# A layer of gated state-space mixing beside a hashed mixture of experts, on one core: chunks transposed from where they lie, GpSimd's tile loop turned round, and the additions of x placed elsewhere

## What is computed

```python
xn = LN(x)                                     # no gain, no bias
# mixing: hidden width 256, state 16
u  = xn @ W_x.T + b_x
g  = sigmoid(xn @ W_g.T + b_g)
u  = u * g + (conv3(u) + conv_b) * (1 - g)     # 3 taps along the sequence
dt = clip(softplus(xn @ W_dt.T + b_dt).mean over all tokens, 0.001, 2)
A  = -softplus(A_raw);  A_d = exp(A * dt);  B_d = (A_d - 1) / (A + 1e-6) * B_ssm
s_t = A_d * s_{t-1} + B_d * u_t;  y_t = sum_s(s_t * C_ssm)
a  = LN(xn + y @ W_out.T + b_out) * ln_g + ln_b
# experts: 8, hidden 512; each token goes to two neighbours, h and h + 1 (mod 8)
h  = int(xn[0] + xn[1]) mod 8
f  = 0.5 * (expert_h(xn) + expert_{h+1}(xn)),  expert_e(v) = relu(v @ W1[e] + b1[e]) @ W2[e] + b2[e]
out = x + a + f
```

## Time and profile before

| | us |
|---|---|
| median of three runs | 494.08 |
| the three runs | 494.71, 491.63, 494.08 |
| the profiled execution, its own time | 491.58 |
| its span, first to last instruction | 489.8 |

### The profile page before, as it was taken

One profiled execution on the slowest core, in us unless ns is written; L12 is line 12 of the kernel. 1 busy time (PEld: TensorE's weight loads), 2 busy tenths in 40 slices (PEclk: granted clock), 3 DMA queues, 4 the chain that ended last, 5 costly groups with the idle time before them and its releaser, 6 DMA issues.

```text
span 489.8 us, 10915 instructions
## 1 busy us (share of the span) xinstructions
PE 423.6 (86%) x3463; PEld 375.1 (77%) x3463; DVE 381.3 (78%) x594; ACT 323.4 (66%) x932; POOL 246.3 (50%) x274
## 2 busy tenths in 40 slices
PE   1056799999889999999999899899999999899940
...
GB/s 237 261 407 324 123 156 181 170 104 141 70 54 32 44 43 43 39 36 43 80 43 43 84 37 132 72 72 43 43 43 33 216 118 152 58 250 148 203 109 128
DMA packets 81254, 56.53 MB, mean 115 GB/s; under 512 B 6178, under 2 KB 74826, under 8 KB 81226
## 3 DMA queue, kind: packets, MB, share of 16 engines
...
## 4 chain that ended last, share of the span: by engine, by line
issue 32%; PE 27%; DVE 12%; DMA 12%; POOL 11%; ACT 3%; POOLq 1%; DVEq 0%; ACTq 0%; SPq 0%
DMA sorted_tokens<-RA,posi 11%; PE PS L1378 8%; POOL AR L580 5%; POOL sorted_tokens L550 3%; PE PS L1445 3%; PE PS L1442 2%; PE PS L1451 2%; DVE RC L1168 2%; PE PS L1361 2%; PE PS L1363 2%; PE PS L1362 2%; PE PS L1428 2%; DVE RC L856 2%; DVE AR L1182 2%; PE PS L1421 1%
## 5 line engine op out<-in xcount | busy, mean ns | idle before, releaser
L1378 PE MATMUL PS<-AR 128*128 128x128 f32 x1184 | 138.5, 275 | 2.3 <-ACT AR L747 2.3
L1378 PEld LDWEIGHTS PS<-AR 128*128 128x128 f32 x1184 | 135.1, 192 | 2.7 <-ACT AR L747 2.7
L747 ACT ACTIVATE AR<-PS,VC 128x256 f32<-128x256 f32 x296 | 112.3, 491 | 10.0 <-PE PS L1363 10.0
L1361 PE MATMUL PS<-XT,RR 128*128 128x256 f32 x296 | 86.2, 291 | 6.5 <-POOL RR L576 3.5
L1363 PE MATMUL PS<-XT,RR 128*128 128x256 f32 x296 | 82.8, 280 | 0.0
L1362 PE MATMUL PS<-XT,RR 128*128 128x256 f32 x296 | 82.5, 279 | 0.0
L556 POOL TENSOR_TENSOR XT<-XTF,XT 128x256 fp32r<-128x256 f32 x37 | 33.3, 900 | 97.8 <-ACT XT L720 97.8
L550 POOL DMA_INDIRECT sorted_tokens<-RA,posi x64 | 61.8, 966 | 23.3 <-issue 13.3
L756 ACT ACTIVATE AR<-PS 128x128 f32<-128x128 f32 x74 | 16.5, 275 | 71.5 <-PE PS L1378 67.8
L580 POOL TENSOR_TENSOR AR<-AR,b2p 128x256 f32<-128x256 f32 x37 | 35.2, 953 | 55.9 <-ACT AR L756 55.6
L1361 PEld LDWEIGHTS PS<-XT,RR 128*128 128x128 f32 x296 | 55.8, 188 | 7.9 <-POOL RR L576 3.9
...
## 6 DMA issues: line engine op xcount, KB each, us to landing
...
AR<-sorted_tokens SPq DMA_DIRECT2D x39, 128.0 KB, 2.1
sorted_outputs<-AR SPq DMA_DIRECT2D x37, 128.0 KB, 1.8
...
```

The lines of the kernel that those rows point to most:

```text
L747: nc.scalar.activation(HID[n][:, k, :], ps[2 * n + k // 2][:, (k % 2) * FT:(k % 2 + 1) * FT], ACT.Relu, bias=B1C[:, e, k:k + 1]).then_inc( ...
L1361: T.matmul(bank, W1h[slot][:, w], XT[:, 0:FT], start=True, stop=False)
L1378: ins = T.matmul(ps[5 + h][:, 0:D], HID[n][:, k, h * P:(h + 1) * P], W2S[slot][:, k, :], start=(n == 0 and k == 0), stop=(n == 1 and k == ...
```

## The change

Line numbers in this section's rows are those of the kernel before or after, as said.

- **Chunks in place.** `transpose_chunk` reads `XN` itself and waits for the norm's pieces; the DMA copies to `xin` are gone, and TensorE's loop over the chunks is written out instead of looped. SyncE's loop only stores chunks, from turn 0 on, and waits for the chunk that it stores to be transposed. The zero tile moves from `RC` to `AR[:, 0:2 * CH]`, where `xin` was, and has 8 blocks, so 11 + 3 clearing DMAs take the place of 9 + 2. ScalarE no longer waits for the clearing; SyncE does, before it loads the first W2. VectorE's `low(1, 0)` goes ahead of the ranking.
- **GpSimd's tile loop.** It does `low_part(i + 1)` first and then the bias; VectorE's `low_tile(1)` is gone, since GpSimd's first turn now makes that part.
- **Exponentials.** `ER` is taken at g = 3 instead of g = 2, with a wait of VectorE's of its own.
- **In-chunk matrix.** In each half of `INTRA`'s rows only the 64 columns of that half are other than zero; it is packed to these 64 columns; the three large memsets become 24 of 512 columns.
- **Gathers.** All are plain, NPL = 4. Batches 4 to 7 go to the half of `RB` that the packing frees, where before 4 to 7 were in the other half; x for batches 0 to 3 is loaded into that same half first, and GpSimd waits for its addition (`s_xb`) before it gathers there.
- **Additions of x and gains.** In the scan stage `add_x` comes at q = 6, 10 and 13 (before at q = 8, 11 and 14); in the tail at g = 2, 3, 7, 11 and 15. `VG` shrinks from six groups to four, so ScalarE scales groups 5 and 9.

```diff
@@ -379,29 +377,23 @@
-            sp.wait_ge(s_nrm, 1)
-            sp.wait_ge(s_nra, 1)
-            for s in range(2):
-                sp.dma_start(xin[s], XN[:, s * TPC:(s + 1) * TPC, :]).then_inc(s_xin[s], 16)
...
-            with sp.Fori(1, NCH // 2) as i:
+            with sp.Fori(0, NCH // 2) as i:
                 for s in range(2):
-                    sp.wait_ge(s_xt[s], i)
-                    sp.dma_start(xin[s], XN[:, bass.ds((i * 2 + s) * TPC, TPC), :]).then_inc(s_xin[s], 16)
+                    sp.wait_ge(s_xt[s], i + 1)
                     sp.dma_start(xn_v[:, bass.ds((i * 2 + s) * TPC, TPC), :], XN[:, bass.ds((i * 2 + s) * TPC, TPC), :]
                                  ).then_inc(s_xnd, 16)
@@ -424,8 +416,9 @@
             sp.dma_start(XSIN, xs_v[0]).then_inc(s_xs, 16)
+            sp.wait_ge(s_fill, 16 * NZ)
+            sp.wait_ge(s_fily, 16 * NY)
             for s in range(2):
-                sp.wait_ge(s_xt[s], NCH // 2)
                 load_w2(s)
@@ -576,10 +569,10 @@
                 with pool.Fori(bounds[g], bounds[g + 1]) as i:
+                    low_part(i + 1)
                     pool.wait_ge(s_ysb, i + 2)
                     nc.gpsimd.tensor_tensor(YSB, YSB, b2p[:, :].rearrange("p (o d) -> p o d", o=1).broadcast_to([P, FH, D]),
                                             ALU.add).then_inc(s_yad, 1)
-                    low_part(i + 2)
@@ -590,15 +583,13 @@
             for n in range(NB8):
-                if n not in PLAIN:
-                    pool.wait_ge(s_xg[n], 16)
-                elif n >= NAR:
-                    pool.wait_ge(s_yps, PPB)
+                if n >= NAR:
+                    pool.wait_ge(s_xb, n - NAR + 1)
...
-                                                 compute_op=ALU.bypass if n in PLAIN else ALU.add).then_inc(s_gat[n], 16)
+                                                 compute_op=ALU.bypass).then_inc(s_gat[n], 16)
@@ -669,8 +660,6 @@
-            act.wait_ge(s_fill, 16 * NZ)
-            act.wait_ge(s_fily, 32)
@@ -731,7 +720,8 @@
-                    nc.scalar.activation(EX, EX, ACT.Exp)
+                    nc.scalar.activation(EX, EX, ACT.Exp).then_inc(s_eexp, 1)
+                if g == 3:
                     nc.scalar.activation(ER, ER, ACT.Exp).then_inc(s_eexp, 1)
@@ -1023,9 +1012,6 @@
-            dve.wait_ge(s_ws, 2)
-            low_tile(1)
@@ -1109,15 +1095,16 @@
-                    ins = V.tensor_copy(IN5[r, hb, :, q, :], TT[r, hb])
+                    ins = V.tensor_copy(IN5[r, hb, :, q % 2, :], TT[r, hb])
@@ -1181,11 +1168,9 @@
-                if q >= DPB and (q - DPB) % 3 == 0 and (q - DPB) // 3 < NPL:
-                    add_x((q - DPB) // 3)
+                if q in (DPB - 2, DPB + 2, DPB + 5):
+                    add_x((q - DPB + 2) // 3)
@@ -1229,8 +1214,14 @@
+                if g == 2:
+                    add_x(3)
+                if g in (3, 7, 11):
+                    add_x(g // 4 + 4)
                 if g + 1 == NT // 4:
+                    scale_gain(13)
                     gain(NB8 - 2)
+                    add_x(NB8 - 1)
@@ -1263,11 +1263,14 @@
             def transpose_chunk(s, i):
-                pe.wait_ge(s_xin[s], (i + 1) * 16)
...
+                pe.wait_ge(s_nrm, q + 1)
+                pe.wait_ge(s_nra, q + 1)
...
-                    ins = T.transpose(ps[s][:, t * P:(t + 1) * P], xin[s][:, t, :], identity[:, :])
+                    ins = T.transpose(ps[s][:, t * P:(t + 1) * P], XN[:, t0 + t, :], identity[:, :])
```

70 lines of the change are left out of this document (31 added, 39 removed).

## The result

Over 20 runs each, the changed kernel takes 491.14 us (median), the kernel before 493.61 us: a ratio of 0.9949, with a 95% interval of 0.9930 to 0.9969. That is 1.5 to 3.5 us faster. One of the changed kernel's 20 runs, 527.01 us at a mean granted clock of 0.845, belongs to a slow state and is left out of the ratio; without it the median is 490.84 us. The forecast was 488.4 us, a gain of 5.65 us; the time is inside the range, but the gain is 2.5 us by the medians and 1.3 us in the profiled pair.

What follows compares the result with a forecast made beforehand. TensorE was taken to bound the kernel until about 375 us, VectorE later, alone from 470.69. Terms +4.7 + 1.6 - 3.1 - 1.0 - 4.0 - 1.0 - 2.85 = -5.65 us gave 488.4 us from 494.08; range 483.5 to 493.0.

Steps and rivals of the forecast that it cites:

- head, to the last chunk: Chunk stage: without the chunk copies and clearing wait, the last chunk's transposes come 2.6 us earlier (bounds 0 and 4.8).
- first sorted tile (from the last chunk on): Before the first sorted tile: SyncE's later loads make TensorE stand 7.3 us, a 4.7 us loss with the head gain included.
- clock behind the stand, to the first tile's products: After TensorE's stand before the first sorted tile: a low granted clock costs 1.6 us (bounds 0 and 3.2).
- tiles 0 to 2: Start of the expert loop: a gain of 3.1 us from tile 0 on, 0.8 if GpSimd's small operations take 4.4.
- boundaries: Between experts: 1.0 us from moving one exponential and 4.0 from GpSimd making the first weights' low part earlier, sum 5.0.
- scan stage: Scan stage: the first of three additions of x moves into VectorE's idle slot, gaining 1.0 us (bounds 0 and 1.2).
- tail: VectorE's last stretch: three additions of x leave (3.8 us), four activations cost 1.0; gain 2.85 (bounds 1.8 and 3.8).
- the next transposes come at 55.4: Head: after ScalarE's high part at 52.8 us, TensorE's next transposes come at 55.4 instead of 57.97 us, gaining 2.6.
- inside the head's slack: Head: the old 4.80 us stand and its 1.6 us clock loss cost nothing, since ScalarE sets the pace there.
- rival (b): Six expert boundaries: GpSimd's new order delays the next low part 1.4 us each, 8.4 in all; 500.8 us, chance 0.08.
- GpSimd releasing TensorE in the middle of the loop: Expert loop: a sign that the forecast is wrong, if VectorE or GpSimd ends TensorE's waits there; no size given.
- the stand at the first tile: Before the first sorted tile's transposes: TensorE idle some 7.3 us, ended by that tile's DMA; under 4 us means wrong.

Runs made afterwards that it cites:

- e2: Changed kernel, but TensorE loads its eight tile bounds before the first sorted tile instead of among the first chunks: 489.76 us, ratio 0.9946 to the kernel before.
- e5: Changed kernel with TensorE's bounds loaded late and chunk 3 transposed twelve times over while TensorE has nothing to do: 490.65 us, ratio 0.9945 to the kernel before.
- e3: Changed kernel without GpSimd's three small operations for the pair's bias, except for the first pair: 489.44 us, ratio 0.9914 to the kernel before.
- e1: Changed kernel, but SyncE loads tile bounds and block counts ahead of its loop of stores instead of behind it: 495.05 us, ratio 1.0037 to the kernel before.
- e7: Changed kernel with the tail's additions of x and the six scale-and-gain groups at their places of before: 492.60 us, ratio 0.9977 to the kernel before.
- e12: Changed kernel with the scan stage's three additions of x back at steps 8, 11 and 14: 493.39 us, ratio 0.9990 to the kernel before.

## Why the prediction was wrong

No step had the wrong sign. The sum promised 4.35 us more than the profiled pair gave, and 3.2 more than the medians of 20 runs; against the 488.4 us forecast, which started from the median of three runs, the median is 2.7 us high. By its steps, forecast against profile:

| step | forecast | measured |
|---|---|---|
| head, to the last chunk | -2.6 | -0.2 |
| first sorted tile (from the last chunk on) | +7.3 | +7.8 |
| clock behind the stand, to the first tile's products | +1.6 | +1.2 |
| tiles 0 to 2 | -3.1 | -3.0 |
| boundaries | -5.0 | -3.2 |
| scan stage | -1.0 | -1.2 |
| tail | -2.85 | -2.75 |
| sum | -5.65 | -1.3 |

Each measured value is the difference of two marks. The first two lines are 107.95 against 108.12, and 12.32 against 4.55 us from there to the first tile. Then come 6.97 against 5.74 us to its products, and 17.97 against 20.94 from there to the third tile's mark. The boundaries are 228.0 against 231.2 from there to the last, the scan stage 63.65 against 64.84 (to the first scales), and the tail 46.22 against 48.97. They sum to -1.3.

**The step that failed first is "the next transposes come at 55.4" in the head.** ScalarE did come at 53.12 (forecast 52.8). I followed ScalarE alone and did not ask what TensorE does in the meantime. It has eight loads of its own there: the stand of 4.80 us gave way to one of 4.46 us behind them, and the low clock that I had written off as "inside the head's slack" now fell on products that were needed. Nor were these loads the only cause, since e2, without them there, stood 5.20 us for ScalarE's and had the low clock too. It cost 1.86 us from the high part on (1.2 in other profiles of the same head), which e5 shows by keeping the clock up. So 1.9 of the 2.4 us missing in the head are this. The wait that was removed here did not take its clock loss with it.

**The second is in the boundaries.** The W1 part's waits went fully (4.2 us of a forecast 4.0), the exponential gave 0.95 of 1.0, as intervals of the tiles. But 2.0 us came back at two boundaries (1.1 in some of the other profiles), where the next low part stood behind small operations and W1 part. That was rival (b)'s mechanism, priced for six boundaries, and one of the prediction's own signs of being wrong, GpSimd releasing TensorE in the middle of the loop. It acted at two of the six. At the first, GpSimd's operations were drawn out beside VectorE's, and e3, without the small operations, has no wait there.

**Right in size, though not what it seemed:** the stand at the first tile. The forecast gave 7.3 us from SyncE's loads and the trace 7.61. The estimate by the Trainium skill (DMA: Bandwidth & Descriptors, Latency and other measured facts), some 0.6 us for each load, would have given 4.8 us; the trace has 5.9 on SyncE again, 0.74 each, above that figure, while TensorE's eight took 4.46, 0.56 each and a little under it. As a term of a sum, however, it misleads: taking it away alone (e1) made the kernel slower. I had written that GpSimd would hold tile 1 to 131 us even without it, but took the price of its small operations at 1.5 us, which is right only while VectorE stands in its own loads. With SyncE early they took 2.8. By the Trainium skill (GPSIMD Engine Reference, Specifications) GpSimd shares its SBUF interfaces with VectorE and contends with it where VectorE has two SBUF inputs. The runs agree: beside such operations 0.30 us became 1.15 (e1) and 1.29 became 2.13 (changed kernel), while beside VectorE's transpose 0.46 stayed 0.46.

**Scan and tail** were right to 0.2 us, and e7 and e12 confirm the terms: three additions off the last stretch give 3.7 us (19.07 against 15.33 from the last scales to the end), and since the whole of that part gives 2.7, the four activations take 1.0. The stretch from the first tile's products to the third tile's mark was right in mechanism too: GpSimd's small operations took 1.4 us (forecast 1.5), and the second tile waited for ScalarE's placing.

**Slips in the working** change no term of the sum: with SyncE's loads at 4.7 us the loss at the first tile would be 3.5, not 3.7 us, and the gain with small operations of 4.4 us would be some 1.0, not 0.8.
